# Output products of a state-space layer in three rounded passes, their left side rounded by ScalarE and split by GpSimd

## The reference

```
z, x, B, C, dt = split(layernorm(h) @ W_in)          # x and z: 4096 wide
x, B, C = silu(causal_conv(x, B, C))                  # 4 taps
dt = softplus(dt + dt_bias);  dA = cumsum(dt * A)     # in chunks of 128 tokens
Y = einsum(C, B, exp(dA_i - dA_j) masked, dt * x)     # inside a chunk
Y = Y + D * x
Y = Y * silu(z)
Y = rmsnorm(Y) * norm_w
h = h + Y @ W_out
```

## Time and profile before

| | |
|---|---|
| median of three runs | 1874.9 us (1874.17 to 1876.9) |
| the profiled execution | 1872.17 us, span 1870.0 us |
| mean granted TensorE clock | 0.955 |
| busy: TensorE | 1655.7 us, 89% |
| busy: weight loads | 1276.5 us, 68% |
| busy: VectorE | 1175.1 us, 63% |
| busy: ScalarE | 931.7 us, 50% |
| busy: GpSimd | 461.8 us, 25% |
| the stage that is changed | from about 1060 to 1542 us of the span |

### The profile page before, as it was taken

The page is one execution under the profiler, slowest core; times in us unless marked ns, Lnnn a source line. Parts: engine busy times, 40 slices in busy tenths (PEclk is TensorE's granted clock), DMA queues, the critical chain, the costliest instruction groups (busy, mean ns, idle before and its releaser), DMA issues. The chain is left out here.

```text
span 1870.0 us, 38238 instructions
## 1 busy us (share of the span) xinstructions
PE 1655.7 (89%) x14220; PEld 1276.5 (68%) x14220; DVE 1175.1 (63%) x2316; ACT 931.7 (50%) x1979; POOL 461.8 (25%) x510
## 2 busy tenths in 40 slices
PE   7988856789999889996688869999999987999898
PEld 4767733558888745663477747777777766888687
DVE  4676688556666622224665588888888875666642
ACT  2455567236656521121255456676766644555552
POOL 2030021023333131221400225454454531000220
PEclk9999978799999999998799889999999998999999
DMA  2020000300000092222000100010101003111000
GB/s 103 3 94 3 4 30 31 117 18 27 26 25 25 18 371 45 47 35 67 14 2 3 50 18 27 26 34 26 34 26 33 27 9 126 35 34 34 1 1 24
DMA packets 27684, 77.91 MB, mean 42 GB/s; under 512 B 2993, under 2 KB 14897, under 8 KB 25393
## 3 DMA queue, kind: packets, MB, share of 16 engines
q1 hardware_dynamic: 23488, 71.19, 11.1%
q0 software_dynamic: 4080, 5.13, 1.7%
HBM read 63.03 MB, written 13.28 MB: 41 GB/s over the span
## 5 line engine op out<-in xcount | busy, mean ns | idle before, releaser
L2662 DVE SCALAR_TENSOR_TENSOR arena<-bank,arena 128x508 f32<-128x508 f32 (+2 forms) x204 | 151.5, 743 | 18.4 <-DVE arena L2662 6.6
L3032 DVE TENSOR_TENSOR L3a_decays<-L3a_decays,L3a_cb_masked 128x512 f32<-128x512 f32 x128 | 94.8, 799 | 49.5 <-ACT L3a_decays L2913 49.5
L2797 PE MATMUL bank<-L3a_wo,L3a_y_gated 128*128 128x256 f32 x512 | 125.0, 388 | 0.0
L2913 ACT ACTIVATE L3a_decays<-bank 128x512 f32<-128x512 f32 x128 | 66.1, 604 | 103.3 <-PE bank L2769 103.3
L2827 PE MATMUL bank<-L3a_xnT_high,L3a_w_high 128*128 128x512 f32 x256 | 105.1, 410 | 1.5 <-ACT L3a_decays L2913 1.5
L2797 PEld LDWEIGHTS bank<-L3a_wo,L3a_y_gated 128*128 128x128 f32 x512 | 91.2, 190 | 21.0 <-issue 11.4
L228 PE MATMUL bank<-const 128*128 128x512 f32 (+1 forms) x154 | 73.7, 619 | 33.7 <-PEq L66 33.7
L2827 PE MATMUL bank<-L3a_xnT_high,L3a_w_low 128*128 128x512 f32 x256 | 100.5, 392 | 0.0
L2827 PE MATMUL bank<-L3a_xnT_low,L3a_w_high 128*128 128x512 f32 x256 | 100.2, 391 | 0.0
L3129 POOL TENSOR_TENSOR arena<-arena 128x1024 f32<-128x1024 f32 x32 | 86.3, 2695 | 44.4 <-ACT arena L2920 44.4
L2064 ACT ACTIVATE arena<-bank 128x512 f32<-128x512 f32 x23 | 13.7, 597 | 145.4 <-PE bank L2013 145.4
(11 more groups left out here) (643 smaller groups left out, 4654.5 us busy)
## 6 DMA issues: line engine op xcount, KB each, us to landing
arena<-in_L3p SPq DMA_DIRECT2D x32, 388.0 KB, 3.0
L1f_experts<-in_L1f SPq DMA_DIRECT2D x8, 1536.0 KB, 18.9
arena<-in_L1x SPq DMA_DIRECT2D x18, 384.0 KB, 3.0
arena<-in_L3x SPq DMA_DIRECT2D x18, 384.0 KB, 3.0
arena<-in_L0f SPq DMA_DIRECT2D x1, 4224.0 KB, 12.9
arena<-in_L3f SPq DMA_DIRECT2D x1, 4055.0 KB, 12.8
rows_sent<-L1a_blank SPq DMA_DIRECT2D x1, 2967.0 KB, 13.6
xnT<-rows_sent SPq DMA_DIRECT2D x23, 129.0 KB, 2.0
```

Of the source, the lines that this page charges most:

```text
L2662: return nc.vector.scalar_tensor_tensor(dst[:, :, d:], psum[:, :, 0:P - d], wcol, dst[:, :, d:], ALU.mult, ALU.add)
L2797: mm = nc.tensor.matmul(ps[g // 2][:, (g % 2) * C:(g % 2 + 1) * C], yg[:, o, g * P:(g + 1) * P], wo[:, o, :], start=False, stop=False, ski ...
L2913: nc.scalar.activation(d4[:, n * HALF:(n + 1) * HALF], bank("d", n)[:, :], ACT.Exp).then_inc(S["diff_read"], 1)
L3032: nc.vector.tensor_tensor(d, d, cbm[:, 4 * half:4 * half + 4, :].rearrange("p b t -> p (b t)"), ALU.mult).then_inc(S["dec_ready"], 1)
```

## The change: what it does

Output products. The gated y of a pair (yg) is split in y_high and y_low, and the scaled output weights wo in wo_high and wo_low. Each of the eight products of a pair becomes three passes of rounded operands. All eight now wait for y_split, which is y_low done. y_high and y_low have one buffer each; wo has one instead of two, wo_high and wo_low have two.

Who makes the parts. ScalarE makes y_high (round_y, a copy of 1024 columns) where it made the squares, and makes the squares behind the second half of z. GpSimd makes y_low (rest_of_y), then adds the squares of one pair earlier than before (j-3 for j-2), then makes wo_high and wo_low (split_output). Its small copy of dt moves to the head of a pair.

Mask tiles. Of the eight output products, five instead of six stand ahead of the differences (the "mask tiles" of L2764 come first in them), and the wait for their banks stands before the fifth. Three stand behind.

Memory. z_dt and abs_dt lie in the tile of cb_masked, and dA_rows in that of xT.

```diff
-        zdt, az, dt, da = (st.sb(n, [P, NB, NH]) for n in ("z_dt", "abs_dt", "dt", "dA"))
+        dt, da = (st.sb(n, [P, NB, NH]) for n in ("dt", "dA"))
+        masked = st.sb("cb_masked", [P, NB * P])
+        zdt, az = (masked[:, n * NB * NH:(n + 1) * NB * NH].rearrange("p (b h) -> p b h", b=NB) for n in range(2))
...
-        wo = st.sb("wo", [P, 2, C])
+        wo = st.sb("wo", [P, C])
+        wo_high, wo_low = (st.sb(f"wo_{n}", [P, 2, C], F32R) for n in ("high", "low"))
+        y_high, y_low = (st.sb(f"y_{n}", [P, TOK], F32R) for n in ("high", "low"))
...
@@ TensorE, output and pair
                     pe.wait_ge(S["wo_ready"], j + 1)
-                    pe.wait_ge(S["y_ready"], j * 2 + half + 1)
+                    pe.wait_ge(S["y_split"], j + 1)
...
-                        mm = nc.tensor.matmul(ps[g // 2][:, (g % 2) * C:(g % 2 + 1) * C],
-                                              yg[:, o, g * P:(g + 1) * P], wo[:, o, :], start=False, stop=False,
-                                              skip_group_check=True)
+                        for a, c in THREE:
+                            mm = nc.tensor.matmul(ps[g // 2][:, (g % 2) * C:(g % 2 + 1) * C],
+                                                  (y_high, y_low)[a][:, g * P:(g + 1) * P],
+                                                  (wo_high, wo_low)[c][:, o, :], start=False, stop=False,
+                                                  skip_group_check=True)
...
-                        output(pe, j - 3, 1 - s, 1, (0, 1), (j, i))
+                        output(pe, j - 3, 1 - s, 1, (0,), (j, i))
...
-                        output(pe, j - 3, 1 - s, 1, (2, 3))
+                        output(pe, j - 3, 1 - s, 1, (1, 2, 3))
@@ ScalarE
+                def round_y(act, j, o):
+
+                    act.wait_ge(S["y_ready"], j * 2 + 2)
+                    act.wait_ge(S["out_done"], j + SLOT_FREE)
+                    nc.scalar.activation(y_high[:, :], yg[:, o, :], ACT.Copy).then_inc(S["y_high"], 1)
...
                     if not early(j):
-                        squares(act, j - 2, s)
+                        round_y(act, j - 2, s)
...
+                        if half == 1 and not early(j):
+                            squares(act, j - 2, s)
...
                 def tail(act):
+                    round_y(act, N - 2, 0)
                     squares(act, N - 2, 0)
+                    round_y(act, N - 1, 1)
                     squares(act, N - 1, 1)
@@ VectorE, skip
-                            dve.wait_ge(S["out_done"], j - 2 + SLOT_FREE)
+                            dve.wait_ge(S["y_split"], j - 2)
@@ GpSimd
-                    nc.gpsimd.tensor_tensor(wo[:, s, :], wo_raw[s], nw[s].to_broadcast([P, C]),
-                                            ALU.mult).then_inc(S["wo_ready"], 1)
+                    nc.gpsimd.tensor_tensor(wo[:, :], wo_raw[s], nw[s].to_broadcast([P, C]),
+                                            ALU.mult).then_inc(S["wo_scaled"], 1)
+
+                def split_output(pool, j, s):
+
+                    pool.wait_ge(S["wo_scaled"], j + 1)
+                    nc.gpsimd.tensor_tensor(wo_high[:, s, :], wo[:, :], k.c["zero"].to_broadcast([P, C]),
+                                            ALU.add).then_inc(S["wo_high"], 1)
+                    pool.wait_ge(S["wo_high"], j + 1)
+                    nc.gpsimd.tensor_tensor(wo_low[:, s, :], wo[:, :], wo_high[:, s, :].bitcast(F32),
+                                            ALU.subtract).then_inc(S["wo_ready"], 1)
+                    pool.wait_ge(S["wo_ready"], j + 1)
+
+                def rest_of_y(pool, j, o):
+
+                    pool.wait_ge(S["y_high"], j + 1)
+                    pool.wait_ge(S["out_done"], j + SLOT_FREE)
+                    nc.gpsimd.tensor_tensor(y_low[:, :], yg[:, o, :], y_high[:, :].bitcast(F32),
+                                            ALU.subtract).then_inc(S["y_split"], 1)
...
                     if not early(j):
-                        add_squares(pool, j - 2)
+                        rest_of_y(pool, j - 2, s)
+                    if not early(j, 3):
+                        add_squares(pool, j - 3)
+                    if not is_first(j):
+                        split_output(pool, j - 1, 1 - s)
 
                 def tail(pool):
                     scale_output(pool, N - 1, 1)
+                    split_output(pool, N - 1, 1)
+                    rest_of_y(pool, N - 2, 0)
+                    add_squares(pool, N - 3)
                     add_squares(pool, N - 2)
+                    rest_of_y(pool, N - 1, 1)
                     add_squares(pool, N - 1)
```

More of the change, by code:

```diff
@@ L2612, in l3_attn @@
         nw = [t[:, at + TAPS + 2:at + TAPS + 3] for t in slot]
-        zdt, az, dt, da = (st.sb(n, [P, NB, NH]) for n in ("z_dt", "abs_dt", "dt", "dA"))
+        dt, da = (st.sb(n, [P, NB, NH]) for n in ("dt", "dA"))
+        masked = st.sb("cb_masked", [P, NB * P])
+        zdt, az = (masked[:, n * NB * NH:(n + 1) * NB * NH].rearrange("p (b h) -> p b h", b=NB) for n in range(2))
         bT, cT = st.sb("bT", [P, TOK]), st.sb("cT", [P, TOK])
-        cbm = st.sb("cb_masked", [P, NB, P])
+        cbm = masked[:, :].rearrange("p (b t) -> p b t", b=NB)
         conv = k.now.spare(2, NB, P)
-        xT = st.sb("xT", [P, 2, TOK])
         sz = k.after.spare(2, TOK)
         dtc = st.sb("dt_pair", [P, 2, NB, 2])
-        wo = st.sb("wo", [P, 2, C])
+        wo = st.sb("wo", [P, C])
+        wo_high, wo_low = (st.sb(f"wo_{n}", [P, 2, C], F32R) for n in ("high", "low"))
+        y_high, y_low = (st.sb(f"y_{n}", [P, TOK], F32R) for n in ("high", "low"))
         dcols = st.sb("d_pair", [P, 2, 1])
-        dax = st.sb("dA_rows", [P, ND, P])
+        xT_and_rows = st.sb("xT", [P, 2 * TOK])
+        xT = xT_and_rows[:, :].rearrange("p (s t) -> p s t", s=2)
+        dax = xT_and_rows[:, :].rearrange("p (a t) -> p a t", a=ND)
         csh = k.after.spare(ND * P).bitcast(F32R)
@@ L2646, in l3_attn @@
             "ms_psum", "zero_set", "dve_step", "d_ready", "x_high", "x_low", "w_high",
-            "w_split", "dA_rows", "dA_rows_act", "cs_psum", "cs_copy", "cs_high", "cs_merged", "cs_left", "cs_rows", "steps_ready", "slot_read", "mask_set", "x_added")}
+            "w_split", "dA_rows", "dA_rows_act", "cs_psum", "cs_copy", "cs_high", "cs_merged", "cs_left", "cs_rows", "steps_ready", "slot_read", "mask_set", "x_added",
+            "y_high", "y_split", "wo_scaled", "wo_high")}
         s_w, s_load = k.now.s_img, k.now.s_slot
@@ L3135, in scale_output @@
                         pool.wait_ge(S["out_done"], j - 1 + SLOT_FREE)
-                    nc.gpsimd.tensor_tensor(wo[:, s, :], wo_raw[s], nw[s].to_broadcast([P, C]),
-                                            ALU.mult).then_inc(S["wo_ready"], 1)
+                    nc.gpsimd.tensor_tensor(wo[:, :], wo_raw[s], nw[s].to_broadcast([P, C]),
[13 more added lines that the diff above has]
+                                            ALU.subtract).then_inc(S["y_split"], 1)
                 def pair(pool, j, s, i):
+                    if not early(j):
+                        pool.wait_ge(S["xt_read"], j * 2 - 2)
+                    hs = slice(j * 2, j * 2 + 2) if isinstance(j, int) else bass.ds(j * 2, 2)
+                    nc.gpsimd.tensor_copy(dtc[:, s, :, :], dt[:, :, hs]).then_inc(S["pair_small"], 1)
                     if not early(j) and s == 0:
@@ L3153, in pair @@
                     if not early(j):
-                        pool.wait_ge(S["xt_read"], j * 2 - 2)
-                    hs = slice(j * 2, j * 2 + 2) if isinstance(j, int) else bass.ds(j * 2, 2)
-                    nc.gpsimd.tensor_copy(dtc[:, s, :, :], dt[:, :, hs]).then_inc(S["pair_small"], 1)
-                    if not early(j):
                         pool.wait_ge(S["y_read"], j * 2 - 2)
@@ L3165, in pair @@
                         pool.wait_ge(S["w_split"], j)
-                        pool.wait_ge(S["wo_ready"], j)
+                        pool.wait_ge(S["wo_scaled"], j)
                         pool.wait_ge(S["d_ready"], j)
```

## The result

The changed kernel takes 1916.7 us (median of 4 runs, 1908.1 to 1920.5) against 1874.5 before: slower by a ratio of 1.0211, 95% interval 1.019 to 1.0232 (the two medians by themselves give 1.0225). The profiled execution took 1919.81 us (span 1918.0), 48.0 more than the span before. E is again the first exponent of a pair of heads.

The account below looks back on a forecast made before the run. TensorE's output products were taken as late, VectorE 0.5 to 0.6 us behind. Intervals 14 x 15.1 + 14 x 13.1 against 379.7 (+15.1), pair 2 to 3 -0.8, tail +7.4: +21.7, forecast 1897 us, range 1867 to 1922.

Parts of the forecast that it names:

- Passes 0.12 apart: TensorE's output products: rounded passes follow each other at 0.120 us, 24 passes a pair taking 2.88 us.
- Intervals alternate, the even pair's fourth weighing falls behind y_low: VectorE's last weighing of even pairs waits for GpSimd's y_low until 5.45; E to E alternates near 15.1 and 13.1 us.
- 0.08 for the signal, the three passes 0.36, differences at 12.01: TensorE's wait for dtx: from the end of dtx to the differences 0.44 us, signal and one product's passes.
- The short interval, 13.1: From an odd to an even pair's first exponent: 13.0 to 13.2 us, taken as 13.1, 14 times.
- the bound by dtx, 12.98: Steady intervals if y_low and the squares don't hold back ScalarE: 12.98 us each, in all 28.
- The long interval, 15.1: From an even to an odd pair's first exponent: dtx at 13.84, differences at 14.28, next E at 15.1 to 15.2.
- Pair 2 to 3, -0.8: The interval with the first output products, 14.50 us before: about 0.8 us less.
- Tail, +7.4: Last pair's E to the mean: 6.1 us more from a chain through one y_high, 1.3 from half clock.
- (1): Rival: the fourth weighing stays ahead of y_low, every steady interval 13.1 us; 1868.6 us, faster; chance 0.19.
- (2): Rival: odd pairs' fourth weighing falls behind y_low too, every steady interval 15.1 us; 1925 us; chance 0.10.
- (3): Rival: TensorE's clock falls to 0.50 in the 15.1 us intervals, +1.3 us in each of 14; 1915; chance in full 0.10.
- (4): Rival: passes don't overlap their weight loads, or gain and tail simply cancel; 1871 to 1879 us; chance 0.09.

Follow-up runs that it names:

- weigh_first: The changed kernel with GpSimd's subtraction for y_low waiting until the pair's four weighings are done: 1893.9 us, ratio to before 1.0104.
- y_low_in_halves: The changed kernel with the subtraction for y_low in two instructions of 512 columns: 1905.0 us, ratio to before 1.0170.
- before_five_three: The kernel before with only the differences moved, behind five output products instead of six, wait ahead of the fifth: 1872.0 us, ratio 0.9983.
- roundings_by_scalar: On top of first_and_late, ScalarE instead of GpSimd rounds the input weights (w_high) and output weights (wo_high): 1876.6 us, ratio to before 0.9996.
- the repeat: The changed kernel as it is, run again on the same chip as the next three: 1912.3 us, ratio to before 1.0195.
- square_late: The changed kernel with ScalarE's square moved from behind the second gate branch's Silu to behind the second x Silu: 1911.0 us, ratio 1.0203.
- first_and_late: The changed kernel with both edits: y_low waits for the four weighings, ScalarE's square stands behind the second x Silu: 1888.1 us, ratio 1.0066.

## Why the prediction was right, and what it mis-sized

The forecast was 1897, range 1867 to 1922; 1916.7 lies inside, on the side of slower that had 0.73. The rise is about 42 us where 22 were forecast. The mechanism is the one it named, but it held by a few hundredths of a microsecond, and several terms were too small. The steps:

- *Passes 0.12 apart*: so they are (1309.64 to 1309.76). Right.
- *Intervals alternate, the even pair's fourth weighing falls behind y_low*: right, place, pair and instruction; weigh_first and y_low_in_halves show it by experiment. That it came out so is in part luck. The prediction had the even pair's weighings begin 1.1 after E and the fourth, by its spacing, near 3.4, well behind y_low at 3.09. They begin 0.63 after E, as before, because the first gate runs ahead of w_high (the steps end at 11.97 and not 11.15); only the end of w_low costs the first weighing 0.24, and the fourth is 0.03 behind y_low. The Trainium skill, "SBUF — State Buffer", section Who interferes with whom, adds that the order of issue decides who blocks, and the other blocks fully; the two outcomes, 0.57 lost by GpSimd or 2.24 by VectorE, agree.
- *"0.08 for the signal, the three passes 0.36, differences at 12.01"*: this term failed. No row showed 0.08 for this wait. From the end of dtx it is 0.33 to the first pass and 0.55 to the differences, 0.88 instead of 0.44. The rows before could have told: there too the differences start 0.95 after dtx ends, and I took that for TensorE being behind with its products. before_five_three shows that the wait on dtx was just as late. That puts 0.44 into each of 28 intervals, 12 us, and leaves hardly any gain from the change's new place for the differences. Why 0.33 is partly to be read: free_for_differences waits for five semaphores one after the other, the steps first. Behind the wait for dtx two more of them follow, behind that for the steps four (0.43), and the trace shows TensorE's queue at work on them until the pass starts. Where a single wait stands right ahead of the matmul it is 0.05 from the second half of x to its transposes and 0.15 from y_low to the last products. No run changed the order of the five waits.
- *The short interval, 13.1*: it is 13.92. From the bound by dtx, 12.98, the term above adds 0.44; the steps end 0.43 after dtx, and behind them TensorE starts 0.43 and not 0.33 later. The prediction had them end at 11.15, and they end at 11.97. Of that 0.8, y_low is 0.2 (2.40 and not 2.18, and 2.72 in odd pairs, where it waits for VectorE first). It was reckoned as twice w_low, but half of y_low takes 1.30 (y_low_in_halves), and w_low with as many columns 1.09. Most of the rest is 0.49 of idle time ahead of the small copy at the head of the even pair, which the sum had at nothing.
- *The long interval, 15.1*: it is 15.62. dtx ends 13.78 after E, forecast 13.84. The prediction's own terms, 13.84 + 0.44 + 0.97, are 15.25 and not 15.1; the 0.44 that failed, less the 0.06, is the rest. Together the intervals are 33.7 us and not 15.1.
- *Pair 2 to 3, -0.8*: +0.5. The failed term is in it too, but more of it is a term put at nothing: w_high starts 7.06 after E where it started 5.56, behind both parts of wo, and dtx ends 1.1 later. With two of these roundings on ScalarE (roundings_by_scalar) the interval is 14.03, 0.5 less than before.
- *Tail, +7.4*: +10.0. The chain is as described (idle 2.85 and 4.24 us). The last y_low ends 26.9 after E, forecast 25.5: GpSimd's row is longer, one sum of squares takes 2.83 beside VectorE's gates. And the half clock cost more: the last 24 passes stand 0.21 apart, 24 x 0.09 is 2.2 for the 1.3 taken. Most of the second product's passes were at half clock as well, but off the path: GpSimd's sum, which stands ahead of the last y_low, ended 0.5 later than the y_high that waited for them.
- *Rivals*: (1) all short, false in 14 intervals, but a hair away: two of 14 came out so in the repeat, three in square_late. (2) all long, false. (3) a clock that falls in the steady part, false (1.00); that its 1915 lies near the measured time is chance. (4) false: the passes do overlap their loads (0.12), and the tail is not cancelled. That ScalarE's square would wait for GpSimd was right (0.61 us idle in a short interval) and harmless until the first bound was gone (square_late against first_and_late).

Not tried: other places for the differences in the changed kernel itself, a wait directly ahead of them, another order of the five waits, and the kernel before with the weights' rounding on ScalarE.

## What to carry to other kernels

Before an operation goes to an engine that is idle half of the time, list what that engine's neighbour does at the moment it will run. Two engines that take turns by whole instructions add up like one. For the one that waits, a long instruction is worse than two of half the length (15.62 against 14.53 here). Where two requests fall within hundredths of a microsecond, say which order is wanted with a wait: here it saved 1.94 us in one interval and cost 0.23 in the next. The time from the last input to the first dependent matmul is to be read off the trace for this very wait, not built from a signal and the work behind it: it was 0.05, 0.15, 0.33 and 0.43 us at four places of one kernel.

## What the runs showed of the hardware

- From the producer's end to the first matmul behind TensorE's wait it took 0.05 us (ScalarE's x to its transposes) and 0.15 us (y_low to the last products) where that wait stood right ahead of the matmul, and 0.33 us (dtx) to 0.43 us (the steps) where further waits of the same list stood behind the one that came last.
- A VectorE instruction with two operands in the on-chip memory waited out GpSimd's whole instruction, of 1.30 and of 2.40 us. Where both started within 0.01 to 0.03 us of each other it was not fixed who went first: one outcome cost GpSimd 0.57, the other VectorE 2.24 us.
- GpSimd took 2.34 to 2.41 us for y_low with 1024 columns and 1.26 to 1.30 for each half of 512. Other operations of 512 columns took less: 1.09 for w_low, 1.04 for w_high, which has one full operand.
- ScalarE rounds 512 columns of weights in 0.63 us and 256 in 0.42, where GpSimd takes 1.04 (1.49 beside VectorE's gate) and 0.61.
